# One fused kernel on Trainium2: at the seam of feed-forward part and attention, the bf16 parts of q and k of batches 0 and 1 are made one step later

## The reference, cut to what matters

```python
gate = fp4_linear(x, w_gate)
h = silu(gate) * fp4_linear(x, w_up)
x = layernorm(x + fp4_linear(h, w_down))
q = rope_rotate((x @ Wq.T).reshape(b, s, 2 * H, D))
k = rope_rotate((x @ Wk.T).reshape(b, s, 2 * H, D))
o = sdpa(q1, k1, vfull) - lam * sdpa(q2, k2, vfull)
```

## Time and profile before

| what | us |
|---|---|
| median of 3 executions | 1060.2 (1057.01 to 1061.86) |
| the profiled execution | 1057.07, of which its span 1055.2 |
| TensorE busy | 914.8 (87% of the span) |
| VectorE busy | 883.0 (84%) |
| GpSimd busy | 787.4 (75%) |
| ScalarE busy | 728.2 (69%) |

### The profile page before, as it was taken

How to read it: one execution, slowest core, us unless ns; L and a number is a source line. 1 busy time by engine, 2 the same in 40 slices (tenths; PEclk the granted TensorE clock), 3 DMA queues, 4 the chain that set the end, 5 groups by cost and what they waited for, 6 DMA issues and landing times. The chain is left out here.

```text
span 1055.2 us, 14663 instructions
## 1 busy us (share of the span) xinstructions
PE 914.8 (87%) x4482; PEld 482.1 (46%) x4482; DVE 883.0 (84%) x1337; ACT 728.2 (69%) x1600; POOL 787.4 (75%) x560
## 2 busy tenths in 40 slices
PE   7697979897989798687777779999999998799995
PEld 2233434342434343234555555566666553355544
DVE  4799999999999999998886477788887873489996
ACT  3776868686868777554565447788788778687871
POOL 2799998989898989885777753667667535677762
PEclk9899999899999999899998899999999999899997
DMA  4762424343343424101500323232332400000001
GB/s 150 321 236 85 202 119 202 120 199 123 139 184 121 176 112 195 40 1 48 100 1 16 104 68 108 80 114 81 104 104 81 118 6 2 0 2 21 10 21 30
DMA packets 35168, 104.03 MB, mean 99 GB/s; under 512 B 3659, under 2 KB 22475, under 8 KB 24395
## 3 DMA queue, kind: packets, MB, share of 16 engines
q1 hardware_dynamic: 35095, 103.16, 28.3%
HBM read 93.84 MB, written 8.91 MB: 97 GB/s over the span
## 5 line engine op out<-in xcount | busy, mean ns | idle before, releaser
L610 PE MATMUL bank<-m_hC,ident 128*128 128x512 f32 x512 | 257.8, 627 | 61.1 <-POOL m_hC L568 22.8
L558 POOL TENSOR_TENSOR m_dBu<-m_du,m_Bt 128x1024 f32<-128x1024 f32 x128 | 299.2, 2353 | 11.7 <-DMA m_Bt<-bcd 11.0
L333 DVE TENSOR_TENSOR_SCAN bank<-bank,m_dBu 128x512 f32<-128x512 f32 x184 | 222.3, 1219 | 16.1 <-ACT bank L461 16.1
L1411 DVE TENSOR_REDUCE a_nm<-bank 128x2 f32<-128x512 f32 x256 | 169.3, 686 | 58.8 <-PE bank L1643 58.4
L610 PEld LDWEIGHTS bank<-m_hC,ident 128*128 128x128 f32 x512 | 93.9, 196 | 203.5 <-issue 111.1
L1580 ACT ACTIVATE late<-bank 128x512 f32<-128x512 f32 x256 | 147.4, 599 | 54.3 <-PE bank L1643 53.5
L461 ACT ACTIVATE bank<-m_delta,early 128x510 f32<-128x510 f32 x256 | 170.0, 677 | 0.3
L342 DVE TENSOR_TENSOR m_hC<-bank,m_Ct 128x512 f32<-128x512 f32 x184 | 123.1, 669 | 0.0
L568 POOL TENSOR_TENSOR m_hC<-m_hS,m_Ct 128x512 f32<-128x512 f32 x72 | 94.4, 1312 | 26.6 <-DVE m_hS L333 26.6
L458 ACT ACTIVATE bank<-m_zero 128x2 f32<-128x2 f32 x181 | 31.2, 173 | 115.1 <-DVE m_hC L342 114.6
L1643 PE MATMUL bank<-qs,ks 99*128 99x256 bf16 x512 | 99.0, 275 | 7.1 <-ACT late L1580 5.8
(11 more groups left out here) (217 smaller groups left out, 1790.7 us busy)
## 6 DMA issues: line engine op xcount, KB each, us to landing
m_Bt<-bcd SPq DMA_DIRECT2D x32, 1024.0 KB, 5.5
m_Ct<-bcd SPq DMA_DIRECT2D x32, 1024.0 KB, 6.4
qs<-parts SPq DMA_DIRECT2D x16, 576.0 KB
ks<-parts SPq DMA_DIRECT2D x48, 192.0 KB
parts<-a_part SPq DMA_DIRECT2D x32, 192.0 KB, 2.3
out<-x_all SPq DMA_DIRECT2D x8, 256.0 KB, 2.3
vx<-in_vrow SPq DMA_DIRECT2D x4, 256.0 KB
qs<-in_fill SPq DMA_DIRECT2D x1, 768.0 KB
```

The source lines that it names most:

```text
L333: nc.vector.tensor_tensor_scan(out, decay, dBu[:, g % RD], 0.0, ALU.mult, ALU.add).then_inc(scan_ready, 1)
L558: nc.gpsimd.tensor_tensor(dBu[:, g % RD:g % RD + CH], du[:, n % 2], Bt[:, s].unsqueeze(1).broadcast_to([P, CH, GTOK]), ALU.mult).then_inc( ...
L610: return nc.tensor.matmul(out, lhsT, rhs, start=start, stop=stop)
L1411: nc.vector.tensor_reduce(nm[:, slot % 2, q, 2 * pair:2 * pair + 2], s1[i % 2][:], AX.X, ALU.max, negate=True).then_inc(max_ready, 1)
```

## The change

For batches 0 and 1 alone, the four operations that make the bf16 parts move out of the step in which q and k are rotated into the next one: L1625 to u = 2, L1510 to u = 3, L1630 to u = 5, L1518 to u = 6. So those of batch 0 are issued in step -3 and those of batch 1 in step -2. Their operands, their semaphores and the waits in them stay as they are, and so does SyncE's stream; `rotate` stays where it is. For the other batches nothing is moved.

```diff
@@ gpsimd body
                 if u == (6 if lone(n) else 10) and has(n, 5):
                     wait(pool, x_turned, n + 5)
                     copy_x(n + 5)
+                if u == 3 and lone(n - 1) and has(n, 3):
+                    residual_high(n + 3)
+                if u == 6 and lone(n - 1) and has(n, 3):
+                    residual_middle(n + 3)
                 if u == (10 if lone(n) else 7) and has(n, 4):
                     rotate(n + 4)
                 if u == (8 if has(n, 4) else 0) and has(n, -3):
                     normalize(n - 3)
-                if u == (13 if lone(n) else 9) and has(n, 4):
+                if u == 9 and has(n, 4) and not lone(n):
                     residual_high(n + 4)
-                if u == (15 if lone(n) else 11) and has(n, 4):
+                if u == 11 and has(n, 4) and not lone(n):
                     residual_middle(n + 4)
@@ scalar body
-                if u == 12 and has(n, 4):
-                    m = n + 4
+                if (u == 12 and has(n, 4) and not lone(n)) or (u == 2 and has(n, 3) and lone(n - 1)):
+                    m = n + (4 if u == 12 else 3)
                     act.wait_ge(rope, 2 * m + 2)
                     wait(act, parts_out, 32 * m)
                     wait(act, split_p, 2 * m)
                     nc.scalar.activation(part[:, 0], rot[:], ACT.Copy).then_inc(split_a, 1)
                 if u == 15 and has(n, -2):
                     squares(n - 2)
-                if u == 15 and has(n, 4):
-                    act.wait_ge(split_p, 2 * (n + 4) + 1)
+                if (u == 15 and has(n, 4) and not lone(n)) or (u == 5 and has(n, 3) and lone(n - 1)):
+                    act.wait_ge(split_p, 2 * (n + (4 if u == 15 else 3)) + 1)
                     nc.scalar.activation(part[:, 1].rearrange("p a t -> p (a t)"), res[:], ACT.Copy).then_inc(split_a, 1)
```

## The result

The changed kernel took 1061.8 us (median of 22 executions, 1059.07 to 1066.67) against 1059.64 us (1056.49 to 1061.86, 22 executions) for the kernel before. The medians differ by 2.2 us. The ratio of the two kernels, taken over all these executions, is 1.0032, with a 95% interval of 1.0020 to 1.0043: 2.1 to 4.6 us slower, and within the 0.5% that I had set as the bound of "same". Forecast: 3.5 us slower, and 1063.7 us as a median, which is 1.9 us above the measured one.

What follows compares the result with a forecast made beforehand. TensorE, busy 87% of the span, was taken to bound the kernel. The 4.2 us gained shrink to 0.3; half clock and waits make L1063 3.5 late: 1057.07 + 3.5 = 1060.6, as a median 1063.7; range 1056.0 to 1067.0.

Steps and rivals of the forecast that it cites:

- Step -4: ScalarE's L1017 no longer waits behind L1625 for the rotation and runs 4.2 us earlier; TensorE keeps full clock.
- Step -3, up to L992: L1075, L928, then GpSimd's L992 at 577.15 instead of 581.56 us; 4.4 us of the gain still there.
- The wait that takes its place: In step -3 ScalarE's second copy waits for L1510 behind L992; of 4.2 us gained, 0.3 is left at L1063.
- TensorE's clock: After over 5 us idle in step -3, TensorE runs at half clock from 583.3, losing 2.35 us (ends 0 and 3.4).
- The loads of batch 0: They land 8.4 us later, about 597.5, stopping TensorE's first maxima; with half clock, no further cost since L934 ends 598.1.
- Step -2: The same wait behind L992 again; L1063 ends at 605.15 instead of 601.60, 3.5 us late.
- The half clock of step -2: Half clock covers over 5.5 us of the work behind L1063, assumed the same length as before.
- Batch 1's transfers: Loads land at 619; the first maxima of batch 1 wait 0 to 1 us, batch 2's L1518 has room; taken as 0.
- The slower one: Half clock lasts through step -3's second half, costing 3.4 instead of 2.35, and longer afterwards; +6.3 us, 1066.5; chance 0.2.
- The one in which nothing is left: The copies wait, but the clock stays full in step -3 and returns sooner in step -2; 1060 within 1; chance 0.18.
- The faster one: The 4.2 us survive because L992 and L1510 come earlier or ScalarE's wait is covered; 1056.0 us; chance 0.12.
- the prize: TensorE's 4.17 us wait for L1017, which stands behind ScalarE's copy L1625 waiting 4.20 us for the rotation.

Runs made afterwards that it cites:

- the cut ahead of L992: Changed kernel with its four moved operations earlier in the next step, so that L1511 is done before L992; ratio to the kernel before 0.9975.
- without its last part: The cut ahead of L992, but with the last subtraction L1519 back at u = 6 as in the changed kernel; ratio to the kernel before 1.0011.
- moving the maxima on the changed kernel: Changed kernel with TensorE's first four maxima of batch 0 behind L1164's transposes and the first q and k product; ratio to the kernel before 1.0051.
- batch 0 alone: Changed kernel with only batch 0's four operations moved, batch 1's in their old places; ratio to the kernel before 1.0018.
- changed with 6 extra products: Changed kernel plus 6 unused products filling TensorE's idle time in step -3, u = 5; ratio to the kernel before 1.0041, five executions.
- the six totals: 12 or 13, then 6, unused TensorE products in the changed kernel, kernel before and best version: 1.0062, 1.0007, 0.9956; then 1.0041, 0.9997, 0.9963.

## Why the prediction was right

**Step -4.** L1017 was to start 4.2 us earlier. It did (5.6 to 1.4 after the mark), and TensorE stayed at full clock there: granted 1.00 from 571 to 575.

**Step -3, up to L992.** Forecast 8.1 us after the mark, measured 8.0, with VectorE's L923 and L934 as the limit.

**The wait that takes its place.** L1063 was to end 0.3 us earlier than before; it was 0.5, with 3.71 us of waiting for L1511. That this wait kept the gain in step -3 is shown by the cut ahead of L992, with and without its last part.

**TensorE's clock.** I took 2.35 us for the half clock between bounds of 0 and 3.4. It was 2.7, 1.8 and 1.9 in three profiles: the price depends on when the clock comes back, and that differs between executions. The rule of the Trainium skill that I weighed ("TensorE: Matmul & The Clock Gate", Part 1: The HAM clock gate), that the throttled state is the default and activity releases it, agrees with this stretch of the trace: by the end of 5.21 us of idleness the level was the lower one.

**The loads of batch 0.** Forecast as late as L934, so free of cost: the first maxima started at 29.01 and L934 ended at 29.14 after the mark. From the end of L1519 they took 12.15 us and not 11.2, since I had read their end off the last busy slice of the transfers and not off the instruction that they release. That moving the maxima on the changed kernel gained nothing bears out that they alone were not the bound.

**Step -2.** Forecast +3.5 at the end of L1063, measured 35.98 - 32.54 = +3.4. This agreement is better than it deserves. The forecast was made for the kind of execution with an early mark; there the changed order with the maxima later, an edit that gains nothing by the argument above, stands at 35.2, so +2.7. With a late mark the old code would stand near 30.2 by my estimate (17.9, and 12.3 from there as before), so there the change costs nearer 5.8. I had not seen that the old wait for the rotation was cover: it hid some 1.7 us (3.8 less 2.1) of VectorE's delay ahead of the seam wherever an execution has that delay, and the change takes this cover away. The 3.4 us of the ratio lie between the two, the 2.2 us between the medians do not; how the executions divide into the two kinds is not known. The half clock of step -2 was an assumption of its own: I took the same 5.5 us of work behind L1063 as before, and in the profile after it was granted 0.50 from about 607 to 610.5, some 3.5 us. That gives about 1 us back that I had not counted, and it too is luck.

**Batch 1's transfers.** This is the term that I mis-sized. I let the first maxima of batch 1 wait 0 to 1 us and L1518 of batch 2 be harmless, and took 0. The maxima waited 0.99 us, half clock set in at the end of that idle time (granted 0.50 from 621 to 624; L1164 took 1.49 us there, 0.87 in the earlier trace rows), and L1063 of step -1 ended 4.5 us late instead of 3.4. The chain of waits goes through these transfers. Other runs tell the parts of this loss from each other. From the end of L1063 in step -2 to these maxima it is 14.5 us after (15.0 before, with its longer half clock), and 13.9 us in two runs in which they wait for no transfer (batch 0 alone; changed with 6 extra products): so the transfers themselves cost 0.6 us. From these maxima to the end of the next L1063 it is 5.3 us after, at half clock, and 3.8 before. But batch 0 alone took 5.4 us there, at half clock too (617 to 619) and without that wait. So whether this half clock came of the transfers stays open.

**The rivals.** The slower one needed the clock to come back later than 588 in step -3 and later than 610 in step -2, which is 18.9 and 40.9 us after the mark. In the profile after it came back at 590.0 and about 610.5, which is 19.5 and 40.0: the first condition held there, the second did not. The one in which nothing is left needed full clock in step -3 (granted 0.50 from 584 to 590) and a whole within 1 us of before, which the interval of 2.1 to 4.6 us excludes. The faster one had GpSimd's order against it; with that order changed, the prize of step -3 is there (10.3 against 14.5).

## What to carry to other kernels

Where several instruction streams are ordered by hand, moving an operation out of one wait puts it behind whatever stands at the new place: look for the longest operation ahead of it on the engine that feeds it, not only at its own engine. Here taking L1625 out of its wait was sound. L1511 ahead of a 3.15 us operation instead of behind it made 3.4 us lost into 1.2 (1.0011, not clear of no change). L1519 ahead of the next such operation, so that its transfers left earlier, made that into 2.6 gained. And one more edit, the first use of a transfer behind work that did not need it, gained another 2.4 us in the seam. Lastly, a wait that is taken away may have covered delays that one profile does not show: read more than one before costing it.

## What the runs showed of the hardware

The granted clock followed idle time with a delay. In the kernel before it fell between 573 and 574, within the idle time that ended at 575.30; but at the next one, from 592.1 to 596.1, it fell only at 597, a microsecond after work had begun again. In the changed kernel with 6 extra products it fell at 582, when TensorE had idled only 1.37 and 0.79 us between 578.4 and 581.4 and was at work again. Filling idle time was no sure way to keep the clock, and none of the six totals in which it was tried shows a clear gain.

With the same code ahead, the mark of the seam lay between 567.5 and 574.8 us in the profiles of all runs, and six of the fourteen are of the late kind. This scatter is larger than the effect measured, which is why single profiles were compared from the mark on, and totals by 5 to 22 executions of each kernel and the interval of their ratio.
